# Second layer of a two-layer convolution kernel: the bias of the two branches written by TensorE, the top branch written transposed, scans that read PSUM, one pooled addition, statistics in another order, group means on 64x64 tiles

## What is computed

```python
p1 = relu(conv3x3(xn, p1_w) + p1_b)           # xn = groups-of-2 normalised x, 64 -> 32 channels
p2 = relu(conv3x3(xn, p2_w) + p2_b)           # 64 -> 32 channels
pool1 = cummax(p1, axis=2, reverse=True)      # running maximum up the rows ("top")
pool2 = cummax(p2, axis=3, reverse=True)      # running maximum to the left ("left")
p   = group_norm(conv3x3(pool1 + pool2, p_w), p_gn_g, p_gn_b)     # 32 -> 64
c1  = group_norm(conv1x1(xn, c1_w), gn1_g, gn1_b)                 # 64 -> 64
out = relu(conv3x3(relu(p + c1), c2_w) + c2_b)
x   = x + out
```

## Time and profile before

| | us |
|---|---|
| median of 3 runs | 151.58 |
| lowest and highest run | 151.33, 152.0 |
| the profiled execution | 151.03 |
| span of its core, first to last instruction | 149.2 |
| start of the second layer's first statistics in that span | 109.55 |
| start of the last convolution | 141.17 |

### The profile page before, as it was taken

One profiled execution on the slowest core, in us unless ns is written; L12 is line 12 of the kernel. 1 busy time (PEld: TensorE's weight loads), 2 busy tenths in 40 slices (PEclk: granted clock), 3 DMA queues, 4 the chain that ended last, 5 costly groups with the idle time before them and its releaser, 6 DMA issues.

```text
span 149.2 us, 3269 instructions
## 1 busy us (share of the span) xinstructions
PE 129.2 (87%) x1395; PEld 111.3 (75%) x1395; DVE 110.5 (74%) x198; ACT 57.4 (38%) x102; POOL 18.5 (12%) x27
## 2 busy tenths in 40 slices
PE   4966399999999899999999998899887999797790
PEld 3654399998898889999899896687655667465460
DVE  5429895095459999799998999998757297965701
ACT  3009539837950768007880128012030317021100
POOL 8941120000000000000018000000003001030100
PEclk9999659999999999999999999999999999999999
DMA  3980000009964000000000000000000000000033
GB/s 95 271 152 0 0 0 4 0 15 256 244 120 108 19 7 0 0 0 4 0 0 0 0 4 0 0 0 4 0 2 4 4 0 4 0 4 0 0 75 70
DMA packets 6672, 5.48 MB, mean 37 GB/s; under 512 B 4656, under 2 KB 5938, under 8 KB 6658
## 3 DMA queue, kind: packets, MB, share of 16 engines
q1 hardware_dynamic: 5986, 4.26, 12.0%
q10 hardware_dynamic: 672, 1.02, 2.7%
HBM read 2.85 MB, written 0.52 MB: 23 GB/s over the span
## 4 chain that ended last, share of the span: by engine, by line
PE 50%; DVE 25%; issue 9%; DMA 6%; ACT 5%; SPq 1%; POOL 1%; POOLq 0%; DVEq 0%
PE bank L990 10%; PE bank L1009 9%; PE bank L982 8%; PE bank L1034 7%; DVE prod L742 7%; DMA prod<-in_w_off 6%; DVE part L769 3%; DVE x_t L861 3%; PE bank L1164 3%; PE bank L1131 3%; PE bank L959 2%; DVE wy L777 2%; DVE pooled L867 2%; DVE bn L580 2%; PE bank L943 2%
## 5 line engine op out<-in xcount | busy, mean ns | idle before, releaser
L742 DVE TENSOR_TENSOR prod<-hat,wy 128x1440 f32<-128x1440 f32 (+3 forms) x25 | 27.3, 1159 | 0.0
L769 DVE TENSOR_TENSOR part<-v,bank 128x1280 f32<-128x1280 f32 (+3 forms) x20 | 21.7, 1109 | 7.1 <-PE bank L1034 3.5
L1009 PE MATMUL bank<-cst,prod 128*128 128x128 f32 (+3 forms) x189 | 22.3, 272 | 0.8 <-DVE prod L742 0.8
L1034 PE MATMUL bank<-cst,part 128*128 128x128 f32 x168 | 21.1, 274 | 1.8 <-DVE part L769 1.4
L1009 PEld LDWEIGHTS bank<-cst,prod 128*128 128x128 f32 (+3 forms) x189 | 20.7, 131 | 1.4 <-DVE prod L742 1.0
L1034 PEld LDWEIGHTS bank<-cst,part 128*128 128x128 f32 x168 | 18.3, 140 | 3.2 <-DVE part L769 3.0
L943 PE MATMUL bank<-ones_r 128*128 128x512 f32 x67 | 18.5, 428 | 2.1 <-POOL w_pair L370 2.1
L990 PE MATMUL bank<-w_cross,g_cross 128*128 128x216 f32 x144 | 19.9, 285 | 0.0
L990 PEld LDWEIGHTS bank<-w_cross,g_cross 128*128 128x128 f32 x144 | 18.6, 203 | 0.0
L982 PE MATMUL bank<-w_pair,g_pair 128*128 128x216 f32 x96 | 15.3, 301 | 3.7 <-ACT g_cross L430 3.7
L943 PEld LDWEIGHTS bank<-ones_r 128*128 128x128 f32 x67 | 13.3, 207 | 4.9 <-POOL w_pair L370 2.1
(11 more groups left out here) (101 smaller groups left out, 154.9 us busy)
## 6 DMA issues: line engine op xcount, KB each, us to landing
v<-v SPq DMA_DIRECT2D x2, 480.0 KB, 6.2
v<-v SPq DMA_DIRECT2D x2, 448.0 KB, 5.9
prod<-in_w_off ACTq DMA_DIRECT2D x1, 486.0 KB, 7.0
prod<-in_w_off SPq DMA_DIRECT2D x1, 486.0 KB, 8.8
w_s<-in_w SPq DMA_DIRECT2D x4, 72.0 KB, 4.4
wc_s<-in_wc SPq DMA_DIRECT2D x2, 144.0 KB, 3.4
wp_s<-in_wp SPq DMA_DIRECT2D x4, 72.0 KB, 2.5
x_b<-in_x SPq DMA_DIRECT2D x1, 256.0 KB, 4.9
```

The source lines that it names most:

```text
L742: return nc.vector.tensor_tensor(prod[:, 0:K2 * CELLS * cx].rearrange("p (k q s) -> p q k s", k=K2, s=cx)[:, q0:q0 + nd], hat[:, c % 2, d0 ...
L769: nc.vector.tensor_tensor(part[:, n % PARTS, 0:nd, 0:cv].rearrange("p d (q e) -> p d q e", e=HD), moved, weights.unsqueeze(3).to_broadcast ...
L1009: last = nc.tensor.matmul(out_ps[0:size, b * P:(b + 1) * P], prod[:, at:at + size], ident, start=(b == 0 and t == 0), stop=(b == n - 1 and ...
L1034: last = nc.tensor.matmul(comb_bank[:, j * P:(j + 1) * P], part[:, n % PARTS, d, j * P:(j + 1) * P], ident, start=(m == 0 and d == 0 and j ...
```

## The change

What it does, part by part:

- **Branch bias.** ACT's `branches` is gone. A new `branch_bias(g)` on PE writes the bias into the PSUM banks (16 matmuls of 256 columns over both rounds; weights `b12_s`, moving operand a column of ones read again and again). The convolutions then accumulate onto it (no `start`). It stands between the two input group means. The dummy matmuls go from 5 and 4 to 4 and 2.
- **Top branch.** Its matmuls (4 of a tap's 8) read the window column by column, so that each next element lies 18 elements (72 bytes) behind the last, and the result lies transposed in PSUM.
- **Scans.** Four of 64x256 for each round, straight from PSUM, with no ReLU ahead of them: the scan multiplies its state by 0 at a row's start and takes the maximum, so it never falls below 0. Their output goes to a tile `maxima` of its own, laid so that one addition of 128x256 makes `pooled`.
- **Statistics.** c1's of both rounds are gathered and have one group mean, one variance, one power and one `affine` over 4 columns. On DVE they are taken behind `pools`, and p's of round 0 stand ahead of c1's variance.
- **Group means.** Six matmuls on 64x64 tiles (two of them add eps) in place of two on 128x128. The variance is one `tensor_scalar` for each image column, with both its scalars read from PSUM, in place of three steps.
- **Second input.** In `both_branches` the shift is computed behind the first addition, no longer ahead of it, and ACT and DVE wait by single images.
- **Loads and stores.** Three more memsets on POOL near the start; four small bias DMAs on SP in place of one; of the last two image columns SP stores the lower halves and ACT the upper ones.

(The last piece begins at the second round's scans.) Nothing of c1's norm stands between the two rounds of scans any more, and all of it stands behind the second. The diff, cut to its core:

```diff
-WARM_IN = (5, 4, 0)
+WARM_IN = (4, 2)
...
+        def norm_cols(s):
+            return HALF if s == G_C1 else DUO
...
+            sp.wait_ge(bias_zero, 2)
+            for row in (0, C):
+                for b in range(2):
+                    sp.dma_start(b12_s[row:row + 1, b * CD:(b + 1) * CD],
+                                 b12[b * C:b * C + CD].rearrange("c o -> o c")).then_inc(ld_vec, 16)
...
-            for n in range(0, HALF, 2):
+            for n in range(HALF):
                 sp.wait_ge(res_ready, n + 1)
-                for half, rows in enumerate((lo, hi)):
-                    sp.dma_start(out_d[n, half], res[rows, n, :]).then_inc(stored, 16)
+                sp.dma_start(out_d[n, 0], res[lo, n, :]).then_inc(stored, 16)
+                if n < DUO:
+                    sp.dma_start(out_d[n, 1], res[hi, n, :]).then_inc(stored, 16)
...
             affine_c(0)
+            second_input(0)
             affine_c(1)
-            second_input(0)
             second_input(1)
-            for n in range(1, HALF, 2):
+            for n in range(DUO, HALF):
                 act.wait_ge(res_ready, n + 1)
-                for half, rows in enumerate((lo, hi)):
-                    act.dma_start(out_d[n, half], res[rows, n, :]).then_inc(stored, 16)
+                act.dma_start(out_d[n, 1], res[hi, n, :]).then_inc(stored, 16)
...
-                link(nc.vector.tensor_copy(sq[:, s, 0:DUO], apart))
-                link(nc.vector.tensor_tensor(sq[:, s, 0:DUO], apart, sq[:, s, 0:DUO], ALU.mult))
-                nc.vector.scalar_tensor_tensor(ab[:, s, 1, 0:DUO], means[:, 1], EPS, sq[:, s, 0:DUO],
-                                               ALU.add, ALU.add).then_inc(var_ready, 1)
+                for j in range(cols):
+                    last = nc.vector.tensor_scalar(ab[:, s, 1, j:j + 1], apart[:, j:j + 1], apart[:, j:j + 1],
+                                                   means[:, 1, j:j + 1], ALU.mult, ALU.add)
+                last.then_inc(var_ready, 1)
...
+                ve.wait_ge(r12_ps, g + 1)
+                both = pair_banks(R12_BANK[g])
+                for b, rows in ((0, lo), (1, hi)):
+                    for r, to in enumerate((lo, hi)):
+                        nc.vector.tensor_tensor_scan(reverse(maxima[to, g, b]), reverse(keep[rows, :]),
+                                                     reverse(both[rows, r]), 0.0, ALU.mult,
+                                                     ALU.max).then_inc(scanned, 1)
+                ve.wait_ge(scanned, 4 * (g + 1))
+                nc.vector.tensor_tensor(pooled[:, g, 1:H + 1, 1:W + 1],
+                                        maxima[:, g, 0].rearrange("p (x y) -> p y x", y=H),
+                                        rows_cols(maxima[:, g, 1]), ALU.add).then_inc(pooled_ready, 1)
...
+                ve.wait_ge(rstd_ready, s + 1)
+                scale = ab[:, s, 2, 0:DUO]
+                link(nc.vector.tensor_scalar(scale, scale, vec_s[:, 0:1], None, ALU.mult))
                 for r in range(2):
+                    n = DUO * g + r
+                    ve.wait_ge(caff_ready, n + 1)
+                    nc.vector.scalar_tensor_tensor(pre[:, n, :], pair_banks(P_BANK[g])[:, r], ab[:, s, 2, r:r + 1],
+                                                   c_aff[:, n, :], ALU.mult, ALU.add).then_inc(pre_ready, 1)
+                    if r == 0:
+                        nc.vector.scalar_tensor_tensor(ab[:, s, 3, 0:DUO], ab[:, s, 0, 0:DUO], -1.0, scale, ALU.mult,
+                                                       ALU.mult).then_inc(norm_ready, 1)
...
+            pools(0)
             c1_stats(0)
-            pools(0)
+            pools(1)
+            link(c1_stats(1))
+            norm_totals(G_C1, HALF)
+            p_stats(0)
             pair_variance(G_C1)
-            c1_affine(0)
-            pools(1)
-            c1_stats(1)
-            p_stats(0)
-            pair_variance(G_C1 + 1)
             pair_variance(G_P)
-            c1_affine(1)
+            affine(G_C1, HALF, vec_s[:, 2:3], vec_s[:, 3:4], vec_s[:, 1:2])
             both_branches(0)
...
+                if s != G_IN:
+                    pe.wait_ge(stats_in, s + 1)
+                for half, rows in enumerate((lo, hi)):
+                    nc.tensor.matmul(stat[rows, 0:2 * cols], cst[rows, C_GB + half * C:C_GB + (half + 1) * C],
+                                     eps_t[rows, 0:cols, :].rearrange("p n t -> p (n t)"), start=True, stop=False)
...
+            def branch_bias(g):
+                for r, rows in enumerate((lo, hi)):
+                    for b in range(2):
+                        for k in range(2):
+                            cols = slice(b * C + k * CD, b * C + (k + 1) * CD)
+                            nc.tensor.matmul(bank[R12_BANK[g] + r][cols, 0:HW], b12_s[rows, b * CD:(b + 1) * CD],
+                                             ones[rows, :].to_broadcast([C, HW]), start=True, stop=False)
...
+            def transposed(tile, rows, n, t):
+                return window(tile, rows, n, t).rearrange("p y x -> p x y")
...
                                 last = nc.tensor.matmul(image(bank[R12_BANK[g] + r][cols, 0:HW]),
                                                         w12_s[rows, t, b * CD:(b + 1) * CD],
-                                                        window(g1, rows, DUO * g + k, t),
-                                                        start=(t == 0), stop=(t == K2 - 1))
+                                                        (transposed, window)[b](g1, rows, DUO * g + k, t),
+                                                        start=False, stop=(t == K2 - 1))
...
             pool_conv(0, {})
-            pool_conv(1, {2: G_C1 + 1, 4: G_P})
-            out_conv(0, {4: G_P + 1})
+            pool_conv(1, {0: G_C1, 3: G_P})
+            out_conv(0, {3: G_P + 1})
```

More of the change, by code:

```diff
@@ L521, in _ @@
             evacuate(NC - 1)
-            def branches(g):
-                act.wait_ge(r12_ps, g + 1)
-                both = pair_banks(R12_BANK[g])
-                if g:
-                    act.wait_ge(scanned, 1)
-                nc.scalar.activation(r12[:, 1], both[hi], ACT.Relu, bias=b12_s[hi, 0:1]).then_inc(r12_ready, 1)
-                if g:
-                    act.wait_ge(scanned, 2)
-                nc.scalar.activation(r12[:, 0].rearrange("p r (x y) -> p r y x", y=H),
-                                     both[lo].rearrange("p r (y x) -> p r y x", x=W), ACT.Relu,
-                                     bias=b12_s[lo, 0:1]).then_inc(r12_ready, 1)
             def affine_c(g):
-                act.wait_ge(norm_ready, g + 2)
+                act.wait_ge(norm_ready, 2)
                 for r in range(2):
-                    last = nc.scalar.activation(c_aff[:, DUO * g + r, :], pair_banks(C1_BANK[g])[:, r],
-                                                ACT.Identity, bias=ab[:, G_C1 + g, 3, r:r + 1],
-                                                scale=ab[:, G_C1 + g, 2, r:r + 1])
-                last.then_inc(caff_ready, 1)
+                    n = DUO * g + r
+                    nc.scalar.activation(c_aff[:, n, :], pair_banks(C1_BANK[g])[:, r], ACT.Identity,
+                                         bias=ab[:, G_C1, 3, n:n + 1],
+                                         scale=ab[:, G_C1, 2, n:n + 1]).then_inc(caff_ready, 1)
             def second_input(g):
@@ L849, in c1_stats @@
                 ve.wait_ge(c_ps, g + 1)
-                norm_stats(G_C1 + g, [pair_banks(C1_BANK[g])[:, r] for r in range(2)])
+                for r in range(2):
+                    last = nc.vector.bn_stats(bn[:, G_C1, DUO * g + r, :], pair_banks(C1_BANK[g])[:, r])
+                return last
             def reverse(ap):
@@ L931, in group_mean @@
             def group_mean(s):
-                pe.wait_ge(stats_in, s + 1)
-                stat = pair_stats(s)
-                nc.tensor.matmul(stat[:, 0:2 * DUO], cst[:, C_GB:C_GB + P],
-                                 mv[:, s, 0:DUO, :].rearrange("p n t -> p (n t)"), start=True, stop=True)
-                nc.tensor.matmul(stat[:, 2 * DUO:], cst[:, C_GD:C_GD + P], mv[:, s, 0:DUO, 0], start=True,
-                                 stop=True).then_inc(stats_ps, 1)
+                stat, cols = pair_stats(s), norm_cols(s)
+                if s != G_IN:
[3 more added lines that the diff above has]
+                                     eps_t[rows, 0:cols, :].rearrange("p n t -> p (n t)"), start=True, stop=False)
+                if s == G_IN:
+                    pe.wait_ge(stats_in, s + 1)
+                for half, rows in enumerate((lo, hi)):
+                    nc.tensor.matmul(stat[rows, 0:2 * cols], cst[rows, C_GB + half * C:C_GB + (half + 1) * C],
+                                     mv[rows, s, 0:cols, :].rearrange("p n t -> p (n t)"), start=False, stop=True)
+                for half, rows in enumerate((lo, hi)):
```

(10 more changed lines are left out.)

71 lines of the change are left out of this document (25 added, 46 removed).

## The result

| | before | after |
|---|---|---|
| median, us | 151.46 | 155.46 |
| lowest and highest | 149.65, 152.0 | 154.72, 156.37 |
| runs | 4 | 4 |
| span of the profiled execution | 149.2 | 152.9 |
| start of the second layer's first statistics in it | 109.55 | 108.48 |

A fourth run of the kernel before, of 149.65 us, stands here beside the three that were known. The ratio is 1.031 (95% interval 1.019 to 1.042). The forecast of 147.4 with a range of 146.0 to 151.6 missed. The time is that of the first rival (155.6), which had been given 0.20. That the two agree to 0.14 us is in part luck: the rival took a gain of 4.2 us for the rest of the change, of which 3.2 came, and the first layer happened to end 1.07 us earlier in the profiled execution.

A forecast was written before the change was run, and what follows sets the result against it. It saw a relay of DVE, PE and the norms as the bound, with PE pausing at three places. Gains of 0.4 + 0.69 + 1.07 + 0.6 + 1.0 + 0.4 made 4.2 us, from 151.58 to 147.4; range 146.0 to 151.6.

The forecast's parts named there:

- the first rival: Branch convolutions: transposed matmuls take twice as long, a convolution 8.2 us, time 155.6; chance of twice or more 0.20.
- the part on the branch convolutions: Both branch convolutions: gain 0.69 us, as a group mean leaves the second; transposed reads assumed to cost nothing.
- The argument against it: Against slow transposed reads on PE: a tile asks for an element every 0.9 ns; four tiles cost no more than two.
- 2.3 ns against 1.15: For slow reads: DVE's addition with a transposed input, per element, against its product of two plain inputs.
- Start: First statistics to first branch convolution: gain 0.4 us, bounds 0 and 0.6; convolution begins at 113.35, not 113.74.
- Branch convolutions: The two branch convolutions: the mean leaves the second one, gain 0.69 us.
- Pooling and p: Pooling: PE's 1.07 us wait goes, four scans 2.45 us; p's second convolution and c1's norm: gain 0.6 us.
- ahead of the mean at 126.6: Before p's second convolution: c1's statistics of both rounds end near 126.3 on DVE, before their group mean at 126.6.
- Within p's second convolution: Two means inside it, costing 1.5 us now, take 0.45 each, 0.9 for both; its end comes 0.6 us closer.
- Between the output convolutions: First to second output convolution: 4.85 us instead of 5.84, gain 1.0; DVE's chain ends last, by 0.3.
- 0.1 us for DVE's queue: Between the output convolutions: steps that DVE's queue may add, named but not put in the 4.85 us.
- End: Last stores, split between ACT and SP with one issue each: gain 0.4 us, bounds 0 and 0.5.

The follow-up runs named there:

- all_transposed: The changed kernel with all eight matmuls of a tap reading transposed, the left branch's too; 155.01 us (one run).
- plain_reads: The changed kernel with the top branch's matmuls reading along the rows again, so its pooling is over the wrong direction; 149.01 us (one run).
- late-mean run: The changed kernel with plain reads, ACT's transposed copy of the top branch to SBUF, and c1's group mean one tap later; 147.98 us, ratio 0.980.
- act_turns_top: The changed kernel with plain reads and ACT copying the top branch transposed from PSUM to SBUF while DVE scans the left; 148.08 us, ratio 0.982.

## Why the prediction was wrong, step by step

The step that failed is the one in the part on the branch convolutions: "That the transposed reads cost nothing is an assumption of this forecast". They cost 3.97 us in the first convolution (8.09 for 4.12) and 4.0 in the second. The mechanism, the factor of two and the side-by-side tiles were worked out correctly as a rival; the weighing was wrong. The argument against it said that an fp32 matmul asks for an element only every 0.9 ns. The runs show that this pace leaves no room for a line an element: two elements in a line held it nearly (4.39 us for 4.04), one halved it (8.07 to 8.38).

The evidence for the rival was two rows of this trace in which other engines pay for such a step. They pay less than the prediction read. ACT's 1.11 for 0.68 us is 1.6 times. DVE's "2.3 ns against 1.15" set an instruction of 256 elements against one of 1440, in which the fixed part of each instruction hardly counts. The same line's shorter products of two plain inputs are the fairer measure:

```profile
L742 DVE TENSOR_TENSOR prod<-hat,wy 128x720 f32<-128x720 f32 x6 | 5.1, 899 | 0.0
...
L742 DVE TENSOR_TENSOR prod<-hat,wy 128x432 f32<-128x432 f32 x4 | 2.2, 599 | 0.0
```

By the straight line through these two, an estimate, 256 plain elements take 0.42 us, so 0.59 is 1.4 times. The rows pointed to a cost, then, but not to the factor of two, and a factor of 1.5 or less would have left the forecast at no change or better. Still, these rows were measurements of such steps; the argument was about a pace that no row had tested against a step. It also took the equal cost of two and four streams (0.451 and 0.458 us a tap) as a sign of slack. That showed only that streams don't share a limit, which all_transposed confirms, and says nothing on how near each is to its own.

The other terms, from the second layer of plain_reads against that of before:

| stretch | gain forecast, us | measured | how it is read |
|---|---|---|---|
| first statistics to first branch convolution | 0.4 | 0.27 | 4.19 to 3.92 |
| first branch convolution to p's first | 0.69 | 0.70 | 9.88 to 9.18 |
| p's first to first output convolution | 1.67 | 1.32 | 11.71 to 10.39 |
| first to second output convolution | 1.0 | 0.79 | 5.84 to 5.05 |
| second output convolution to the end | 0.4 | 0.14 | 8.03 to 7.89 |
| sum | 4.2 | 3.22 | 39.65 to 36.43 |

- **Start.** The bias (1.10 us for 0.92) and the dummies lay in the wait as forecast, and the convolution started 0.20 us behind PE's last mean, on DVE. The mean for the first group took from 109.58 to 110.02, 0.44 us (0.4 taken). The variance took until 110.61, when DVE began the next statistics, 0.59 us where 0.5 was taken; this makes most of what is missing.
- **Branch convolutions.** The mean that left was worth what it cost, 0.69.
- **Pooling and p.** The pause of 1.07 us went, as forecast. The scan was mis-sized: 2.83 us for four in place of 2.45. With it c1's aggregates came behind the mean that PE takes ahead of tap 0, and PE waited 0.43 to 0.45 us there. So "ahead of the mean at 126.6", with 0.3 us to spare, failed. The late-mean run takes the wait away and shortens this stretch by 0.13 us only (121.73 to 132.13 in act_turns_top, 122.85 to 133.12 without the wait), so even correct scans would have let the chain of DVE and POOL decide.
- **Within p's second convolution.** The two means made it 0.74 us longer in plain_reads (128.38 to 133.18, less the 4.06 of a convolution without a mean), where 0.9 was taken. POOL's power over four columns took 1.01 us (1.02 taken), four variance steps 0.84 (0.75), two 0.48 (0.5).
- **Between the output convolutions.** The order of what ends last was right (DVE's chain, PE idle 0.58 us where 0.3 was forecast). Hand-overs of 0.03 to 0.1 us between PE, DVE and POOL make the 0.2 us; the prediction had named 0.1 us for DVE's queue and not put it in.
- **End.** One store less on ACT did not bring the end closer by 0.4. Rows of the last stores of the changed kernel, SP first:

```profile
149.69 1.11 SPq L361 DMA_DIRECT2D out<-u  x2
149.69 1.39 ACTq L555 DMA_DIRECT2D out<-u  x2
```

ACT's two issues begin at the third result and take 1.39 us beside SP's two, longer than the 0.57 each of the median in the earlier trace rows. They end 1.93 us behind the convolution (151.08 less 149.15). Before, the last issue ended 2.09 us behind it (147.41 less 145.32). The split brought 0.16, and the sum had priced its issues too low.

The account closes: 8.0 lost and 3.2 gained make a loss of 4.8, and the second layer grew from 39.65 to 44.42 us.

## What to carry to other kernels

Before an operand is turned by its access pattern, look at how far apart its elements lie: on PE a step of 16 or of 72 bytes in SBUF halved the pace of an fp32 read, and two slow matmuls in eight set the time of the whole tap. Turn it where an engine is idle or on the way into PSUM, which cost 0.4 us or less in place of 8 (second layers of 36.47 and 36.79 us against 36.43 with plain reads). Compare rows of like length before you read a price per element from them. When rows of the trace speak for a rival and only an argument speaks against it, give the rows the larger chance.

## What the runs showed of the hardware that was not expected

- The cost of a stepped fp32 read on PE roughly follows the share of elements that begin a new line of 16 bytes: records of 375 ns plain, 395, 515 and 634 ns at steps of 8, 12 and 16 bytes. The plain matmuls beside them in other tiles kept 380 to 385 ns.
- A write in steps of 64 bytes into PSUM, by half of the matmuls, did not slow the pace of an fp32 convolution (4.12 us for the second).
- A `tensor_tensor_scan` of 256 elements took 0.71 us, a pair of 512 2.30 us. Halving the length saved less than half, and PSUM as source was no slower than SBUF (1.41 and 1.40 us for two).
- The first layer's end moved by 2.3 us between two executions of the same first layer, in the changed kernel (108.48) and in plain_reads (110.77), and the place of PE's low clock explains it. The share of the full clock that was granted, in 40 slices, plain_reads first:

```profile
PEclk9999955999999999999999999999999999999999
```

```profile
PEclk9986999999999999999999999999999999999999
```

In plain_reads PE had stood still for 3.68 us up to 17.44 us, and the clock was at its lower level (0.5 of full, that is 1.2 of 2.4 GHz) from about 19 to 25.8 us, on the first layer's convolutions. In the changed kernel PE had stood still for 1.51 us up to 9.53 us, and the clock was at that level from about 10.6 to 14 us, on dummy matmuls. The same nine matmuls, plain_reads first:

```profile
19.54 2.23 PE L1000 MATMUL bank<-w_cross,g_cross 128*128 128x216 f32 x9 [0.54 <-DVE w_cross L723]
```

```profile
19.76 1.23 PE L1000 MATMUL bank<-w_cross,g_cross 128*128 128x216 f32 x9 [0.53 <-DVE w_cross L723]
```

The fourth group of nine, at full clock in both, began at 27.28 and 25.00 us. So the 2.3 us were lost by then, and from there to the end the two run alike. In all thirteen profiled executions the layer ended at 108.3 to 109.0 us where the mean granted clock was 0.984 to 0.989, and at 109.1 to 110.8 where it was 0.974 to 0.977.
